# An attention and expert kernel on Trainium2: the mixed rows turned one unit later, without the constants multiplied ahead of them, and both output products in unit 15

## What is computed

```
gate = jax.nn.sigmoid(local @ gl_w + remote_h @ gr_w)
mixed = gate * local + (1.0 - gate) * remote_h
mixed = mixed.transpose(0, 2, 1, 3).reshape(B, S, D)
return mixed @ out_w + out_b
```

## Time and profile before

| what | value |
|---|---|
| median of 3 runs | 1847.35 us (1846.54 to 1850.95) |
| the profiled execution | 1851.47 us, span 1849.7 us |
| mean granted TensorE clock | 0.979 |
| PE busy over the span | 1739.9 us, 94% |
| DVE, ACT, POOL busy | 68%, 54%, 50% |
| PE busy in 650 to 700 us | 47.91 of 50 us |

### The profile page before, as it was taken

How to read it: one execution, slowest core, us unless ns; L and a number is a source line. 1 busy time by engine, 2 the same in 40 slices (tenths; PEclk the granted TensorE clock), 3 DMA queues, 4 the chain that set the end, 5 groups by cost and what they waited for, 6 DMA issues and landing times.

```text
span 1849.7 us, 39539 instructions
## 1 busy us (share of the span) xinstructions
PE 1739.9 (94%) x13056; PEld 1424.9 (77%) x13056; DVE 1252.8 (68%) x3077; ACT 996.1 (54%) x2312; POOL 926.4 (50%) x1113
## 2 busy tenths in 40 slices
PE   5999999999999999997999998999999999989996
PEld 3666666666666666655888887999999999978886
DVE  7778888888888888876676665533333333358787
ACT  2566667776776676666333335444444444435554
POOL 3345555555555555555278765555555555401101
PEclk8899999999999999998899999999999999999999
DMA  6655566655556655543164312233222222257875
GB/s 120 94 76 93 102 107 127 104 103 103 107 94 104 116 106 104 92 102 102 61 151 89 82 48 66 77 77 88 75 76 75 75 75 75 69 196 180 206 209 98
DMA packets 164114, 189.79 MB, mean 103 GB/s; under 512 B 41777, under 2 KB 121970, under 8 KB 163922
## 3 DMA queue, kind: packets, MB, share of 16 engines
q1 hardware_dynamic: 136642, 142.92, 37.0%
q0 software_dynamic: 24976, 43.41, 9.2%
q10 hardware_dynamic: 2304, 0.93, 0.3%
HBM read 84.87 MB, written 51.40 MB: 74 GB/s over the span
## 4 chain that ended last, share of the span: by engine, by line
PE 72%; DVE 8%; ACT 7%; issue 6%; POOL 5%; DMA 1%; ACTq 1%; SPq 0%; POOLq 0%; DVEq 0%
PE bank L496 5%; PE bank L497 5%; PE bank L498 5%; PE bank L1636 5%; PE bank L2514 5%; PE bank L2512 5%; PE bank L2513 5%; PE bank L1693 4%; PE bank L1658 4%; PE bank L1638 4%; PE bank L1637 4%; ACT prob L1074 3%; PE bank L2533 3%; PE bank L2534 3%; PE bank L2535 3%
## 5 line engine op out<-in xcount | busy, mean ns | idle before, releaser
L924 POOL TENSOR_SCALAR_AFFINE_SELECT prob<-prob 128x512 f32<-128x512 f32 x256 | 162.8, 636 | 382.3 <-ACT prob L1074 382.2
L1074 ACT ACTIVATE prob<-bank 128x512 f32<-128x512 f32 (+1 forms) x512 | 248.8, 539 | 103.2 <-PE bank L1680 100.5
L2405 DVE TENSOR_TENSOR b_h<-b_h,bank 128x352 f32<-128x352 f32 x135 | 70.3, 521 | 283.9 <-ACT b_h L2347 283.9
L2329 POOL DMA_INDIRECT y_scratch<-b_y,names x135 | 134.1, 993 | 180.2 <-ACT b_y L2360 177.1
L1399 DVE COPY_PREDICATED bank<-from_prev,bank 128x512 f32<-128x512 int32 x192 | 133.0, 693 | 98.0 <-PE bank L1658 94.1
L1402 DVE TENSOR_REDUCE row_max<-bank 128x4 f32<-128x512 f32 x256 | 177.3, 693 | 26.8 <-PE bank L1658 19.5
L2347 ACT ACTIVATE b_h<-bank 128x352 f32<-128x352 f32 x135 | 62.6, 464 | 212.0 <-PE bank L2514 212.0
L2512 PE MATMUL bank<-wgu_h,bxT_h 128*128 x540 | 175.8, 326 | 0.8 <-DVE wd_l L2429 0.8
L2513 PE MATMUL bank<-wgu_l,bxT_h 128*128 x540 | 175.5, 325 | 0.0
L2514 PE MATMUL bank<-wgu_h,bxT_l 128*128 x540 | 175.1, 324 | 0.0
L1693 PE MATMUL bank<-prob,v_sb 128*32 128x256 f32 (+1 forms) x2048 | 159.3, 366 | 0.0
(11 more groups left out here) (357 smaller groups left out, 5242.4 us busy)
## 6 DMA issues: line engine op xcount, KB each, us to landing
kS<-qk_h SPq DMA_DIRECT2D x128, 128.0 KB, 4.0
qS<-qk_h SPq DMA_DIRECT2D x128, 128.0 KB, 5.7
f_y<-y_scratch SPq DMA_DIRECT2D x16, 1024.0 KB, 9.1
x_in<-in_L_attn_x_dram SPq DMA_DIRECT2D x16, 512.0 KB, 6.2
kS<-qk_l SPq DMA_DIRECT2D x64, 128.0 KB, 4.8
qS<-qk_l SPq DMA_DIRECT2D x64, 128.0 KB, 6.7
x_res<-in_L_attn_x_dram SPq DMA_DIRECT2D x16, 512.0 KB, 4.0
out_dram<-x_res SPq DMA_DIRECT2D x16, 512.0 KB, 5.1
```

Source lines behind the costliest of these rows:

```text
L924: op = e.affine_select(out=own, in_=own, compare_op=ALU.is_gt, fill=0.0, base=0, pattern=[[0, HG], [1, P]], channel_multiplier=-1)
L1074: e.activation(prob[:, u % SLOTS, 2 * hp:2 * hp + 2, 0:w], src[:, :, 0:w], ACT.Exp, scale=SCALE).then_inc(keyed.frees[hp], 1)
L2329: e.indirect_dma_start(out=y_dram, out_offset=bass.IndirectOffsetOnAxis(ap=b_names[:, b, 1:2], axis=0), in_=b_y[:, b % 2, :], in_offset=No ...
```

## The change

`turn_mix` and `mix_high` move from units 12 and 13 to units 13 and 14, `mix_low` from 13 and 14 to 14 and 15. `turn_mix` no longer calls `keep_busy` (its other calls stay). `project_out` of the first half moves from unit 14 to unit 15, ahead of the product with the values; the second half and the second half of the latent scores move behind that product. On PE in unit 13 the row maxima are turned ahead of the mixed rows, on ACT `minus_max` stands ahead of `mix_high`.

```
@@ ACT, body
                         if u == 12:
-                            if live(prev):
-                                mix_high(prev, 0)
                             if live(i):
                                 latent_out(i)
                             if live(before):
                                 normed(2, before, x_res, (0, 1))
+                        if u == 13 and live(nxt):
+                            minus_max(nxt, 1 - buf, 0)
+                        if u in (13, 14) and live(prev):
+                            mix_high(prev, u - 13)
                         if u == 13:
-                            if live(prev):
-                                mix_high(prev, 1)
-                            if live(nxt):
-                                minus_max(nxt, 1 - buf, 0)
                             if live(before):
                                 normed(2, before, x_res, (2, 3))
@@ DVE, body
-                        if u in (13, 14) and live(prev):
-                            mix_low(prev, u - 13)
+                        if u in (14, 15) and live(prev):
+                            mix_low(prev, u - 14)
@@ PE
                 def turn_mix(i, p):
                     name = f"mix{p}"
                     pe.wait_ge(*front.drained(i, name))
-                    if p == 0:
-                        keep_busy(name, 3)
                     pe.wait_ge(mixed_ready, 2 * i + p + 1)
...
-                        if u in (12, 13) and live(prev):
-                            turn_mix(prev, u - 12)
                         if u == 13 and live(nxt):
                             turn_max(nxt, 0)
+                        if u in (13, 14) and live(prev):
+                            turn_mix(prev, u - 13)
                         if at(i, SEQS) and u == 13:
...
-                        if u in (14, 15):
-                            if live(prev):
-                                project_out(prev, u - 14)
-                            if live(nxt):
-                                latent_scores(nxt, u - 14)
+                        if u == 14 and live(nxt):
+                            latent_scores(nxt, 0)
+                        if u == 15 and live(prev):
+                            project_out(prev, 0)
                         if u % T == LAG:
                             weigh(i, prev, buf, u)
+                        if u == 15:
+                            if live(prev):
+                                project_out(prev, 1)
+                            if live(nxt):
+                                latent_scores(nxt, 1)
```

## The result

| | before, on the same chip | changed |
|---|---|---|
| median | 1849.15 us (1846.54 to 1851.07, 4 runs) | 1867.09 us (1863.35 to 1873.02, 4 runs) |
| ratio | | 1.0107, 95% interval 1.0091 to 1.0123 |
| the profiled execution | 1851.47 us, span 1849.7 | 1873.02 us, span 1871.3 |
| mean granted clock | 0.979 | 0.965 |

By the ratio the change makes the kernel 1.1% slower; the medians lie 17.9 us apart. The profiled execution shows 21.6 us more.

The account below looks back on a forecast made before the run. PE's end bounds the kernel, with DVE's row maximum setting the pace in units 11 to 13. Exchange -1.3, last call +2.2 and clock +5.0 sum to +5.9 us: profiled 1857.4, median 1853.3 us, range 1843 to 1862.

Parts of the forecast that it names:

- The hole: PE, unit 12: idle 1.28 us without constants and first turn; unit 13 starts 0.06 behind DVE's maximum, 0.26 earlier.
- Units 13 and 14: PE: no wait for POOL at the turns, unit 14 0.65 us earlier; the 0.24 wait for ACT's exponentials goes.
- Unit 15's wait for ACT: PE, ahead of unit 15's keyed scores: a new wait of 0.51 us for ACT's exponentials of unit 14.
- The exchange: Per sequence: constants and waits removed against DVE's remaining hole and late ACT; -0.10 us, over 13 sequences -1.3 us.
- some 1.9 us of constants and waits: The time per sequence that the prediction said the change takes away, of which the exchange keeps 0.10 us.
- The last call: ACT's copy and table load come later, delaying the expert's activation: +2.2 us, bounds 0 and 2.2.
- The clock: Emptier stretch around the hole lowers PE's granted clock: 5 falls among 13 sequences at 1.0 us each, +5 us; chance 0.53.
- The rival of falls in every sequence: Clock falls in all 13 sequences: 1886 us at sequence 0's length, 1866 with shorter falls; chance 0.12.
- The clock holds: Rival: no clock falls in the attention part, sum +0.9 us, 1848.2 us; chance 0.23.
- ACT is in time: Rival: no ACT wait in unit 15, exchange worth 0.61 us a sequence, 7.9 us in all; 1839.4 us; chance 0.12.

## Why the prediction was right or wrong

**The hole** (unit 12): right. PE idle 1.21 for 1.28, unit 13 0.06 behind the maximum. That spreading DVE's work shrinks it to 0.7 shows whose it is.

**Units 13 and 14**: right. No wait for POOL or ACT there; the plain scores of unit 14 start 2.30 behind unit 13's start (404.93 - 402.63), as worked out (446.50 - 444.20).

**Unit 15's wait for ACT**: right at 0.52 for 0.51, and confirmed by moving `normed`, which removes it. The exchange that it is part of was wrong in sign: +0.24 us a sequence instead of -0.10, +3.3 us instead of -1.3. From unit 13's start to the next sequence it is 11.34 (402.63 to 413.97) for the 11.03 of the sum: the keyed product behind the wait starts 0.12 late and takes 0.37 where I had 0.26 from the earlier trace rows, and the output half 1.87 where I had 1.78. Together 0.31, two of the three being durations that I had read where other work stood around them. Less the 0.07 that the hole is shorter, this turns -0.10 into +0.14; the last 0.1 I can't place. (The "some 1.9 us of constants and waits" is 1.68 by the earlier trace rows: 1.12 from the constants to the first turn, 0.32 and 0.24. No sum uses it.)

**The last call**: +1.8 for +2.2, with the table load where I put it and the activation 2.5 later. PE meets it as 1.78 us more of waiting for DVE's `member`. That it reaches the end of the kernel is not shown.

**The clock**: the step that failed. "I take 5" falls at "1.0 of it" gave +5; there were 8, which cost 13.5, or 1.7 each. The mechanism was right: constants back take the falls away, and constants out of the kernel before bring them. The size was not. A long fall costs 2.1 (53.08 - 51.00), nearer my upper bound of 2.9 than the 1.0 I took: I had taken half of sequence 0's length because the work behind the hole is dense, but five of the eight lasted as long as sequence 0's, 6.8 us, and in the kernel before without constants they lasted 10.2. Sequence 0's own fall, which I had left out as unchanged, grew by 1.5 us, perhaps by chance. Of the 15.7 us between the +5.9 of the sum and the +21.6 of the profile, the falls are 8.5 (13.5 - 5.0), the exchange 4.6, sequence 0 1.5 and the expert part behind the last call 2.7, less 0.4 for the last call and 1.2 for the stretch ahead of it. The rival of falls in every sequence had 1866 us for the short ones, near the measured 1867.09, but by luck: there were 8 falls behind 13 holes, not one behind each, and most of them long ones.

**The rivals.** "The clock holds" fell: there were eight falls between 100 and 800 us, none of them behind a single wait over 1.22 us. The Trainium skill ("TensorE: Matmul & The Clock Gate", "Why this matters for your kernels") names a single gap longer than that as what brings the clock down; by it this rival would have been the outcome, and the trace disagrees. "ACT is in time" fell as a forecast, yet its price was about right: 0.61 then, 0.75 when `normed` was moved. With nine transposes in the hole no fall came. The Trainium skill (same title, "Part 4: PE-mode transpose") says that transposes do not count as work for the clock in the way matmuls do; this run disagrees.

## What to carry to other kernels

Before filler is taken out, ask what its hole would do to the clock: here products that no one reads cost nothing (50.74 us a sequence with, 50.77 without them) and in the changed order held off 16.7 us. If it is to go, first close the hole by moving the waited-for engine's other work behind what is waited for, and count by how much the next engine in line (here ACT, 0.5 us) comes late. An order that is slower alone can still make the room: with DVE and ACT rearranged around it, it gave 1823.11 us.

## What the runs showed of the hardware

- The same hole does not always bring the clock down: 1.21 us ahead of 402.63 and ahead of 453.63, and only behind the second did it fall. With 13 holes each of 1.21, 1.16 and 1.22 us there were 8, 5 and 8 falls in a profiled execution, with 0.78 one, with 0.7 and 0.32 none; one execution each, so the counts are no rates.
- Sequence 0's stretch, with the same code and a wait of about 0.6 us, fell in the kernel before (0.62 of full clock from 90 to 99 us) and held in the one without constants and in the one with constants behind the hole (1.00 from 85 to 100 us in both). With one constant it held behind a single wait of 1.35 us (ahead of 90.92; 1.00 from 85 to 102 us). One stretch that fell or held is weak ground for a count, as I used it.
- Dense work behind a fall does not end it at once: the constants behind the hole ran at the lower level, 1.42 us for three from 400.73 to 402.15 in one sequence (0.50 of full clock from 400 to 403 us).
- What stays open: why one hole and not the next is followed by a fall, whether the wait of 0.44 us ahead of unit 12 has a part in it (no kernel here loses that wait and keeps the whole hole), and how the count spreads over executions; the medians and the mean granted clocks of the other executions cover it only as a sum.
